# Eight smallest keys from one max operation, and the first x in two halves on two queues, in a categorical matmul kernel

## The reference

```python
selected_W = W[cat_ids]
selected_b = b[cat_ids]
y = jnp.einsum('bti,bio->bto', x, selected_W) + selected_b[:, None, :]
return x + y
```

## Time and profile before

| | |
|---|---|
| median of 3 runs | 361.41 us (361.26 to 361.68) |
| profiled execution | 361.15 us |
| its span, first to last instruction | 359.3 us |
| granted TensorE clock | 1.000 of full speed |
| PE busy | 354.5 us, 99% of the span |
| DVE, ACT, POOL busy | 48%, 41%, 75% |

### The profile page before, as it was taken

How to read it: one execution, slowest core, us unless ns; L and a number is a source line. 1 busy time by engine, 2 the same in 40 slices (tenths; PEclk the granted TensorE clock), 3 DMA queues, 4 the chain that set the end, 5 groups by cost and what they waited for, 6 DMA issues and landing times.

```text
span 359.3 us, 6835 instructions
## 1 busy us (share of the span) xinstructions
PE 354.5 (99%) x1554; PEld 289.7 (81%) x1554; DVE 172.3 (48%) x278; ACT 146.8 (41%) x262; POOL 268.3 (75%) x147
## 2 busy tenths in 40 slices
PE   8999999999999999999999999999999999999996
PEld 3788888888888888888888888888888888888884
DVE  6564454544544544454454454455445445445442
ACT  4563354434433443443443344344344344334420
POOL 3687999998648698799964999799979799934000
PEclk9999999999999999999999999999999999999999
DMA  5999999999887998989997899899998999855532
GB/s 198 327 402 377 383 361 299 332 375 332 336 300 244 368 318 290 301 301 384 329 323 258 287 377 328 273 338 369 332 326 292 368 346 314 317 203 189 188 117 89
DMA packets 43381, 109.51 MB, mean 305 GB/s; under 512 B 4817, under 2 KB 4818, under 8 KB 38610
## 3 DMA queue, kind: packets, MB, share of 16 engines
q1 hardware_dynamic: 37730, 70.01, 53.9%
q0 software_dynamic: 5328, 38.28, 31.4%
q10 hardware_dynamic: 288, 0.79, 0.7%
HBM read 75.50 MB, written 33.55 MB: 304 GB/s over the span
## 4 chain that ended last, share of the span: by engine, by line
PE 98%; DMA 1%; DVE 0%; issue 0%; ACT 0%; SPq 0%
PE pA L429 96%; PE pA L383 1%; DMA xs<-xt 1%; DVE os L376 0%; ACT xh L292 0%; DVE tbc L336 0%; SPq L149 0%; PE pA L400 0%; DVE fill L315 0%; PE pS L393 0%; PE pS L392 0%; SPq L150 0%; SPq L154 0%
## 5 line engine op out<-in xcount | busy, mean ns | idle before, releaser
L376 DVE TENSOR_TENSOR os<-pA,bb 128x512 f32<-128x512 f32 x128 | 88.5, 691 | 170.6 <-PE pA L429 169.7
L292 ACT ACTIVATE xh<-xs 128x512 fp32r<-128x512 f32 x127 | 80.4, 633 | 195.6 <-PE pA L429 125.5
L265 POOL TENSOR_TENSOR wl<-wr,wh 128x2048 fp32r<-128x2048 f32 x30 | 138.7, 4625 | 2.5
L429 PE MATMUL pA<-wh,xh 128*128 x508 | 136.1, 390 | 0.4 <-ACT xh L292 0.4
L429 PE MATMUL pA<-wl,xh 128*128 x508 | 135.8, 390 | 0.0
L429 PE MATMUL pA<-wh,xl 128*128 x508 | 135.8, 390 | 0.0
L429 PEld LDWEIGHTS pA<-wh,xh 128*128 128x128 f32 x508 | 95.3, 188 | 20.3 <-issue 0.8
L429 PEld LDWEIGHTS pA<-wh,xl 128*128 128x128 f32 x508 | 95.4, 188 | 19.9 <-issue 0.3
L429 PEld LDWEIGHTS pA<-wl,xh 128*128 128x128 f32 x508 | 95.4, 188 | 19.8
L341 DVE TENSOR_TENSOR xl<-pT,xh 128x512 fp32r<-128x512 f32 x127 | 86.6, 682 | 10.8 <-ACT pT L295 10.8
L261 POOL TENSOR_SCALAR wh<-wr 128x2048 fp32r<-128x2048 f32 x30 | 57.6, 1921 | 36.3 <-PE pA L429 34.4
(11 more groups left out here) (50 smaller groups left out, 19.7 us busy)
## 6 DMA issues: line engine op xcount, KB each, us to landing
xs<-xt SPq DMA_DIRECT2D x128, 256.0 KB, 5.4
out<-os SPq DMA_DIRECT2D x128, 256.0 KB, 5.0
wr<-w POOLq DMA_DIRECT2D x29, 1024.0 KB, 7.3
bb<-bias POOLq DMA_DIRECT2D x7, 1024.0 KB, 9.6
wr<-w SPq DMA_DIRECT2D x2, 512.0 KB, 5.8
wr<-w SPq DMA_DIRECT2D x1, 1024.0 KB, 9.0
wr<-w ACTq DMA_DIRECT2D x1, 512.0 KB, 3.8
bb<-bias SPq DMA_DIRECT2D x2, 256.0 KB, 7.5
```

The lines of the kernel that those rows point to most:

```text
L265: eng.tensor_tensor(wl[:, at], wr[:, c % NR, :], wh[:, at].bitcast(f32), ALU.subtract).then_inc(s_wp if c == 2 else s_w, 1)
L292: eng.activation(xh[:, i % NH, :, :], xs[:, i % NX, :, :], ACT.Copy).then_inc(s_xh, 1)
L376: eng.tensor_tensor(os[:, i % NO, :], pA[i % NA][:, :], bb[:, bass.ds(at, D)], ALU.add)._wait_ge(s_mm, i + 2).then_inc(s_fin, 1)
L429: mm = eng.matmul(pA[i % NA][:, :], xp[:, i % NH, k, :], wp[:, bass.ds(at + k * D, D)], start=(n == 0), stop=(n == 3 * KT - 1))
```

## The change

VectorE now forms keys that fall where the old ones rose (`rev` is 4095 minus the number, from which 128 times the category is taken), in float32, and one `max` operation gives the eight largest in falling order: the first eight batches in sorted order. SP takes the numbers of x 0 to x 7 from these eight values and waits for the table only ahead of its loop. x of batch 0 is loaded in two halves of 64 partitions, one from SP and one from ACT, so the waits for buffer 0 count 16 more. The tables of SP, POOL and VectorE load eight registers at a time, PE's four as before. The two arms of the If on PE are swapped. POOL has one more iota.

```diff
-        key = sb("key", [1, 128], i32)
-        low1 = sb("low1", [1, 1], i32)
+        rev = sb("rev", [1, 128], f32)
+        key = sb("key", [1, 128], f32)
+        top = sb("top", [1, 8], i32)
...
-        def table(eng, name, src, n, lo, hi, ahead=4):
+        def table(eng, name, src, n, lo, hi, ahead=8):
...
-        def x_load(eng, i, b):
-            eng.dma_start(xs[:, i % NX, :, :], xt[b, :, :].rearrange("a p (k t) -> (a p) k t", k=KT))\
+        def x_load(eng, i, b, p0=0, p1=128):
+            eng.dma_start(xs[p0:p1, i % NX, :, :], xt[b, p0:p1, :].rearrange("a p (k t) -> (a p) k t", k=KT))\
                .then_inc(s_x[i % NX], 16)
+
+        def x_landed(eng, i):
+            eng.wait_ge(s_x[i % NX], 16 * (i // NX + 1 + (i % NX == 0)))
...
-            first = eng.alloc_register("first")
+            first = [eng.alloc_register(f"first{i}") for i in range(8)]
+
+            def sorted_first(i):
+                return (B - 1) - eng.snap(first[i], min_val=0, max_val=C * B - 1) % B
+
             eng.wait_ge(s_t0, 1)
-            eng.load(first, low1[0:1, 0:1])
-            x_load(eng, 0, bass.ds(eng.snap(first, min_val=0, max_val=C * B - 1) % B, 1))
+            eng.load(first[:2], top[0:1, 0:2])
+            x_load(eng, 0, bass.ds(sorted_first(0), 1), 0, 64)
             eng.dma_start(raw(0, 3, KT), W[0, :, 3 * D:]).then_inc(s_w0[2], 16)
-            eng.wait_ge(s_tab, 1)
             ahead = table(eng, "la", tbc, B, 0, B - 1)
             behind = table(eng, "st", tbc, B, 0, B - 1)
-            ahead(0)
 
             def load(i):
-                b = ahead(i)
+                b = sorted_first(i) if i < 8 else ahead(i)
...
             load(1)
             w1_load(0)
+            eng.load(first[2:], top[0:1, 2:])
             load(2)
...
             bias_load(eng, 1, 2, s_b0[1])
+            eng.wait_ge(s_tab, 1)
             for i in range(B):
...
         def _(eng):
+            eng.iota(rev[:, :], [[-1, 128]], base=C * B - 1, channel_multiplier=0,
+                     allow_small_or_imprecise_dtypes=True).then_inc(s_io, 1)
...
             eng.activation(spare[:, :], ones[:, 0:1], ACT.Copy)
+            first = eng.alloc_register("second")
+            eng.wait_ge(s_t0, 1)
+            eng.load(first, top[0:1, 0:1])
+            x_load(eng, 0, bass.ds((B - 1) - eng.snap(first, min_val=0, max_val=C * B - 1) % B, 1), 64, 128)
...
-            link(eng.scalar_tensor_tensor(out=key[:, :], in0=idr[:, :], scalar=float(B), in1=iot[0:1, :],
+            link(eng.scalar_tensor_tensor(out=key[:, :], in0=idr[:, :], scalar=-float(B), in1=rev[:, :],
                                           op0=ALU.mult, op1=ALU.add))
-            eng.tensor_reduce(low1[:, :], key[:, :], AX.X, ALU.min).then_inc(s_t0, 1)
+            eng.max(top[:, :], key[:, :]).then_inc(s_t0, 1)
...
-            row = table(eng, "wo", tbc[1:2, :], B, 1, C)
+            row = table(eng, "wo", tbc[1:2, :], B, 1, C, ahead=4)
...
-            with eng.If_lt(lowest, B):
-                eng.wait_ge(s_x[0], 16)
+            with eng.If_lt(lowest, (C - 1) * B):
+                eng.sem_inc(s_raw, 1)
+                one = eng.alloc_register("one")
+                eng.wait_ge(s_tab, 1)
+                eng.load(one, tbc[1:2, 0:1])
+                batch(0, eng.snap(one, min_val=1, max_val=C), early)
+            with eng.Else():
+                x_landed(eng, 0)
...
-            with eng.Else():
-                eng.sem_inc(s_raw, 1)
-                one = eng.alloc_register("one")
-                eng.wait_ge(s_tab, 1)
-                eng.load(one, tbc[1:2, 0:1])
-                batch(0, eng.snap(one, min_val=1, max_val=C), early)
             eng.wait_ge(s_tab, 1)
```

More of the change, by code:

```diff
@@ L280, in _ @@
             eng.activation(spare[:, :], ones[:, 0:1], ACT.Copy)
+            first = eng.alloc_register("second")
+            eng.wait_ge(s_t0, 1)
+            eng.load(first, top[0:1, 0:1])
+            x_load(eng, 0, bass.ds((B - 1) - eng.snap(first, min_val=0, max_val=C * B - 1) % B, 1), 64, 128)
             def high_0(k0, k1, done):
-                eng.wait_ge(s_x[0], 16)
+                x_landed(eng, 0)
                 eng.activation(xh[:, 0, k0:k1, :], xs[:, 0, k0:k1, :], ACT.Copy).then_inc(done, 1)
             def high(i):
-                eng.wait_ge(s_x[i % NX], 16 * (i // NX + 1))
+                x_landed(eng, i)
                 if i == NH:
@@ L327, in _ @@
             link(eng.tensor_copy(colf[:, :], pS[:, 128:129]))
-            eng.wait_ge(s_io, 4)
+            eng.wait_ge(s_io, 5)
             link(eng.scalar_tensor_tensor(out=cmp[:, :], in0=pS[:, 0:128], scalar=colf[:, 0:1], in1=dif[:, :],
@@ L397, in _ @@
             eng.wait_ge(s_t0, 1)
-            eng.load(lowest, low1[0:1, 0:1])
+            eng.load(lowest, top[0:1, 0:1])
             eng.wait_ge(s_hot, 2)
```

## The result

| | before | after |
|---|---|---|
| median of 7 runs | 361.28 us (361.10 to 361.68) | 362.64 us (362.23 to 362.82) |
| ratio | | 1.0035 (95% interval 1.0025 to 1.0044) |
| profiled execution, its span | 361.15, 359.3 us | 362.23, 360.4 us |

The changed kernel is 0.35% slower, 1.36 us, where I had forecast 0.38 us less. Later measurements gave the kernel before medians of 361.2 to 361.6 us, with single runs up to 362.5; each experiment is read against the kernel before measured beside it.

A forecast was written before the change was run, and what follows sets the result against it. PE's matmuls bound the kernel, with other work deciding only before 9.97 us. Terms -0.23 - 0.20 + 0.05 = -0.38 us gave a forecast of 361.0 us, own range 360.7 to 361.4, with rivals 360.3 to 361.8.

The forecast's parts named there:

- x of batch 0 in halves: First x load, split over SP and ACT: landing between 5.8 and 6.5 us, covered, so 0.0 (0 to +0.2).
- x of batches 1 to 5: SP's next x loads, no longer waiting for the table: 2 us earlier, so x 1 stops holding up batch 1.
- the PE queue: In-order register work behind batch 0 limits batch 1; without branch (0.18) and x 1 wait (0.05), start 9.74, gain 0.23.
- the gaps behind batch 1: PE's matmuls from batch 1 to 2: batch 2 follows without a gap, gain 0.08 + 0.12 = 0.20 us.
- The max: VectorE's max with eight results replaces the minimum: 0.32 instead of 0.27 us, +0.05 (from -0.07 to +0.28).
- x 1: Batch 1's load on SP: issued about 4.4 to 4.5, transit 3.2, landing 7.7 us; x 2 issued near 5.7.
- C: Rival, chance 0.07: ACT's half of x 0 lands beyond 6.5 us, 0.3 to 1.0 net lost, 361.3 to 362.
- B: Rival, chance 0.10: POOL, given W[1]'s half early, collides with VectorE; 0.6 to 1.2 us lost, 361.6 to 362.2.
- A: Rival, chance 0.20: array's own end of batch 0 decides, not PE's queue; batch 1 at about 9.45, 360.3 to 360.6.

The follow-up runs named there:

- e1: Changed kernel with x of batch 0 in one transfer from SP again; 361.79 us, ratio 1.0017.
- e3: Changed kernel with both halves of x 0 issued by SP, one behind the other; 363.08 us, ratio 1.0055.
- e10: Changed kernel with three more dummy matmuls before batch 0; 362.44 us, ratio 1.0031.
- e2: Changed kernel, halves kept, with SP's wait for the table back ahead of x 1; 362.92 us, ratio 1.0040.
- e5: e1 with the half of W[1] held back until the table is there, x 1 still early; 362.27 us, ratio 1.0018.
- e4: e1 with the two arms of the If in the order of the kernel before; 361.95 us.
- e15: e1 with x 1 held back until x 0 has landed; 363.45 us, ratio 1.0041.
- e6: e1 with the last quarter of W[0] issued by ACT at the start; median of six 362.77 us, ratio 1.0046.
- e11: e6 plus three dummy matmuls, last quarter of W[0] on SP behind the ids, one register loaded before x 0; 361.02 us, ratio 1.0004.
- e13: e11 with x 1 held back until POOL's flag and two added dummy matmuls instead of three; 361.64 us, ratio 1.0002.
- e7: Changed kernel, halves kept, with the last quarter of W[0] issued by ACT at the start; 363.83 us, ratio 1.0071.
- e8: Kernel before with only the last quarter of W[0] issued by ACT at the start; 361.88 us, ratio 1.0021.
- e14: e13 without any added dummy matmul; 361.55 us, ratio 1.0004.

## Why the prediction was wrong

- **The step that failed** is "x of batch 0 in halves", **0.0** (0 to +0.2), together with the start of "x of batches 1 to 5": I followed x 0 and x 1 to their landings and never priced the transfer between them. The quarter had no slack in the trace before. ScalarE was done with the third quarter near 7.5 (6.91 and half of 1.17), just when POOL had finished the last (6.95 + 0.46), and in the changed kernel, e1, e3 and e10 batch 1 began 2.7 us behind POOL's start on it (8.82 and 11.49, 8.04 and 10.78, 9.47 and 12.14, 8.99 and 11.66). From POOL's end the distance is 2.20 to 2.22 us in these four and in e2 and e5 too, whose operation was longer, and 2.46 in e4, which has the branch back. In the trace before POOL was done at 7.41; plus 2.46 that is 9.87, so the quarter had 0.10 us of slack before the 9.97. The end moved by 1.87; less 0.10 of slack and 0.24 for the branch that is gone, that makes 1.53 of the measured 1.52.
- **Its size, in parts.** POOL's start moved from 6.95 to 8.82, 1.87 us. 0.36 is SP's longer way to x 0 (3.73 against 3.37; shown in e1 with a whole x; I had 0.1), 0.20 the longer issue of a half (0.59 against 0.39). The transit grew by 1.31: 0.7 of it is what follows, x 1 and the half of W[1] (3.87 in e1 against 3.20 in e15; x 1 alone 0.46, e5), about 0.5 the halves (3.68 in e2 against 3.20), and 0.1 is left over. These parts come from single executions, with a spread of up to 0.16 between like kernels. Of the 1.87, some 0.7 belongs to the halves, 0.7 to the early followers and 0.4 to the registers.
- **Right: the PE queue.** The branch that the swap of the arms takes away is worth 0.24 in the traces of e1 and e4, where I had 0.18. With the quarter out of the way (e6) batch 1 started at 9.87, where I had 9.74: there the array's own end of batch 0 at 9.83 decided.
- **Right: the gaps behind batch 1.** Two batches take 17.04 - 11.49 = 5.55 us instead of 5.79; I had 5.56. The max is +0.01 instead of +0.05.
- **Half right: x 1.** It was issued at 5.43, not 4.5, for the same reasons as the quarter, and was no longer what batch 1 waited for. But its own transit was 3.9 us, not 3.2: issued 0.95 earlier than before, it landed near 9.3, later than before (9.04). The half of W[1], issued 0.94 earlier, took 5.5 instead of 4.3 and landed later too. So in the changed kernel the early issues gained nothing in landing time. x 2 went out at 7.94, not near 5.7: the load of six registers in front of it took 1.29 us (L191). It was in time all the same.
- **The rivals.** C, the ACT half late, came nearest, but not by its mechanism: PE began batch 0 at 6.83, later than the 6.5 allowed. Batch 0 takes 3.21 us from there to its small matmul (6.20 to 9.41 before, 6.62 to 9.83 in e6), so even with the quarter in time it would have ended at 10.04, 0.3 past the forecast 9.74 (an estimate); beside the quarter this didn't count. B (POOL and VectorE) failed in its premise: the half of W[1] was no earlier than before, and POOL began on it at 11.44. The table tv took 1.06 us (L377) and ended just behind POOL's L249 (12.26 + 1.11), but delayed nothing. A didn't occur in the changed kernel, where the array waited for the quarter; in e6, e11 and e13 batch 1 did start 0.04 us behind the small matmul, as A has it, but with x 0 late. No rival's price reached the 362.64; C's own ends at 362, below the 362.13 for which the range counted its far part.
- **The rule I set aside.** The Trainium skill (page "DMA: Bandwidth & Descriptors", section "Rules for kernel authors") says not to split a transfer into halves of the partitions, since they share the engines. The runs agree that nothing is won and go further: it cost some 0.7 us on two queues, and with both halves on one queue the two issues and the register operations between them took 1.50 us instead of 0.39 (e3). Whether the halves ran one after the other, as the page has it, no run separates.
- **Not settled.** Why a follower slows the transfer ahead of it. The engines moved 131 GB/s at a busy share of 0.8, so packets took longer than in the trace before, and no run here shows what held them. And whether the clock explains the times above 361.9 in e6 and e11: e7 shows it in the granted clock, e3, e8 and e14 only in the length of the passes, and no execution of that group of e6 or e11 left a trace.

## What to carry to other kernels

When a change moves transfers on a queue, list every transfer between the first and the last one that moves, and ask of each when it must land: the one that nobody changed was the one with no slack. Early loads are not free while a critical transfer is under way: here x 1, issued 0.8 us behind it, and the next load behind that cost it 0.7 us, and were themselves in no sooner than before. And don't split a load in two for latency before you have priced the issue of the second half and what stands behind it.

## What the runs showed of the hardware

- Issuing half of x (64 partitions, 128 KB) took 0.56 to 0.59 us on each of two queues, and 0.59 and 0.49 for two on one queue, where the whole (256 KB) took 0.38 or 0.39.
- POOL's operation on the quarter took 0.46 us by itself and 0.94 in e2 and 0.74 in e5, where it overlapped an operation of VectorE.
- In the changed kernel, register loads from the eight keys took 0.47 us for one (ACT, L293), and on SP 0.67 for two and 1.29 for six, while a load of eight from the table took 0.53 (L150). Queue instructions by line, ns min/median/max:

```profile
L293 ACTq TENSOR_LOAD <-top x1: 473/473/473, 2.7 to 2.7; - x1
...
L174 SPq TENSOR_LOAD <-top x1: 674/674/674, 2.7 to 2.7; - x1
...
L150 SPq TENSOR_LOAD <-tbc x31: 520/529/1142, 14.2 to 337.2; - x31
...
L191 SPq TENSOR_LOAD <-top x1: 1287/1287/1287, 6.3 to 6.3; - x1
```

- The first 10 us don't run at one speed in every execution. In e7 the granted clock fell from 2.4 to 1.2 GHz after 1.85 us without matmuls. In the traces of the changed kernel, e1, e3, e8 and e14 the column says 1.00 over the first 16 us, but the lengths do not agree with it. The same two dummy matmuls, of 512 and 256 columns, took 0.50 to 0.65 us in some traces and 0.82 in others, here in e14 and in the changed kernel:

```profile
3.62 1.67 PE L395 MATMUL pA<-fill 128*128 128x512 bf16 x4
...
5.53 0.82 PE L395 MATMUL pA<-fill 128*128 128x512 bf16 x2
```

```profile
5.53 0.50 PE L397 MATMUL pA<-fill 128*128 128x512 bf16 x2
```

  All seven traces with 0.82 for the two (e1, e3, e4, e5, e8, e14, e15) have longer raw passes behind them: 2.08 to 2.41 us in e1, e4, e5 and e15, and 3.51 to 3.78 in e3, e8 and e14. All the others but e7 have 1.88 to 1.99. In e3, e8 and e14 the next matmul starts 2.79 to 2.80 us after the first raw one, in the changed kernel 1.42: twice the time, as at the lower of the two levels. So the long passes look like a rise of the clock that came late, some time between 5.5 and 10 us, not like a fall; that it is the clock is inferred from the lengths, since the column doesn't show it. Until 5.5 us PE did the same work in these and in the changed kernel (0.2 later in e8), and the four dummies from 3.62 took 1.67 in them, where e6, e10 and e11 have 1.24 to 1.31. Before x 0 it stood idle for 0.43 to 0.86 us in e3, e8 and e14 and for 0 to 0.27 in the other four, but for 0.80 in the changed kernel too, whose passes were short, so the idle time alone does not sort them. Batch 1 began 1.89 us later in e14 than in e13, and the groups of runs lie 2.0 (e6) and some 1.6 us (e11) apart.
